# Second layer: the first 17 tiles listed from three sequences' counts, the last sequence routed within the stage; the prologue reordered; integers kept as integers in the rows

## The reference

```python
x = x + 0.5 * moe(layernorm(x))      # 8 experts, top 2 per token
x = x + lru(layernorm(x))            # complex diagonal recurrence over the sequence
x = x + 0.5 * moe(layernorm(x))

def moe(x):
    logits = x @ router_w.T + router_b
    topk_val, topk_idx = top_k(logits, 2)
    weights = softmax(topk_val)
    # expert e: h = x @ w1[e].T + b1[e]; h1, h2 = split(h); (silu(h1) * h2) @ w2[e].T + b2[e]
    return sum over the two chosen experts of weight * expert(x)
```

## Time and profile before

| | us |
|---|---|
| median of 3 runs | 672.25 (671.88 to 679.42) |
| the profiled run | 666.18, its span 664.4 |
| prologue, until the first expert matmul | 99.9 |
| first layer's tiles | 188.5 |
| recurrence and routing | 156.8 |
| second layer's tiles | 188.9 |
| outputs of the second layer | 30.3 |

### The profile page before, as it was taken

One profiled execution on the slowest core, in us unless ns is written; L12 is line 12 of the kernel. 1 busy time (PEld: TensorE's weight loads), 2 busy tenths in 40 slices (PEclk: granted clock), 3 DMA queues, 4 the chain that ended last, 5 costly groups with the idle time before them and its releaser, 6 DMA issues.

```text
span 664.4 us, 16357 instructions
## 1 busy us (share of the span) xinstructions
PE 462.8 (70%) x4580; PEld 408.6 (61%) x4580; DVE 423.0 (64%) x1336; ACT 350.9 (53%) x798; POOL 333.4 (50%) x463
## 2 busy tenths in 40 slices
PE   2433007888899999971988783327879799999910
PEld 2433005676699988860878673216769599989910
DVE  6563564656689996737799384145546477776715
ACT  4656233555577777752253431325457477877720
POOL 1277683545656655560002657604557556565640
PEclk9999999879899999985889786558889799999975
DMA  6142362333323222206000101102333223232228
GB/s 195 53 144 72 113 155 63 73 78 80 65 56 67 60 56 52 60 15 227 27 0 18 49 24 56 50 16 61 80 75 84 61 63 69 53 56 61 54 67 313
DMA packets 94552, 50.17 MB, mean 76 GB/s; under 512 B 81902, under 2 KB 84720, under 8 KB 94484
## 3 DMA queue, kind: packets, MB, share of 16 engines
q1 hardware_dynamic: 85396, 32.31, 20.3%
q0 software_dynamic: 9088, 16.94, 8.0%
HBM read 17.25 MB, written 23.24 MB: 61 GB/s over the span
## 4 chain that ended last, share of the span: by engine, by line
PE 55%; DVE 18%; issue 13%; DMA 5%; ACT 3%; another core or an unknown queue 3%; SPq 1%; POOL 1%; POOLq 0%; DVEq 0%; ACTq 0%
PE bank L1188 11%; PE bank L1189 11%; PE bank L1190 11%; PE bank L1210 5%; PE bank L1208 5%; PE bank L1209 5%; DMA yin<-y 3%; DVE bn L658 2%; DVE xres L909 2%; ACT xn L462 2%; PE bank L1070 1%; PE bank L1202 1%; PE bank L1168 1%; DVE w1l L786 1%
## 5 line engine op out<-in xcount | busy, mean ns | idle before, releaser
L424 POOL DMA_INDIRECT y<-yout,dest x156 | 155.3, 995 | 142.3 <-ACT yout L549 105.7
L993 DVE SCALAR_TENSOR_TENSOR act<-bank,bias,gate 128x256 f32<-128x256 f32 x312 | 146.3, 479 | 105.0 <-ACT gate L531 86.6
L403 POOL DMA_INDIRECT rows<-rows,slot_i x128 | 136.2, 1064 | 149.9 <-DVE slot_i L745 110.2
L1188 PE MATMUL bank<-xt_t,w1h 128*128 128x256 f16 x624 | 176.1, 282 | 26.9 <-DVE w2l L786 13.0
L531 ACT ACTIVATE gate<-bank,bias 128x256 f32<-128x256 f32 x312 | 142.3, 479 | 89.1 <-remote 56.0
L1190 PE MATMUL bank<-xt_t,w1l 128*128 128x256 f16 x624 | 175.7, 282 | 4.9 <-issue 4.9
L1189 PE MATMUL bank<-xt_t,w1h 128*128 128x256 f16 x624 | 175.8, 282 | 4.6 <-issue 4.3
L1210 PE MATMUL bank<-w2h,actl 128*128 x624 | 123.5, 223 | 5.8 <-issue 5.8
L1208 PE MATMUL bank<-w2h,wst 128*128 x624 | 124.9, 223 | 3.5 <-issue 3.0
L1209 PE MATMUL bank<-w2l,wst 128*128 x624 | 123.5, 223 | 2.7 <-issue 2.7
L999 DVE TENSOR_TENSOR actl<-act,wst 128x512 f16<-128x512 f32 x156 | 107.8, 691 | 15.2 <-ACT wst L539 10.3
(11 more groups left out here) (200 smaller groups left out, 552.9 us busy)
## 6 DMA issues: line engine op xcount, KB each, us to landing
yin<-y SPq DMA_DIRECT2D x16, 512.0 KB, 4.8
wst<-in_w_t SPq DMA_DIRECT2D x8, 512.0 KB
y<-yout,dest POOLq DMA_INDIRECT x156
rows<-padrow SPq DMA_DIRECT2D x18, 130.0 KB
xres<-in_x SPq DMA_DIRECT2D x8, 256.0 KB, 3.4
wst<-in_w_t SPq DMA_DIRECT2D x8, 256.0 KB
rows<-rows,slot_i POOLq DMA_INDIRECT x128
out<-xres SPq DMA_DIRECT2D x4, 512.0 KB, 6.8
```

What stands on the lines that cost most here:

```text
L403: pool.indirect_dma_start(out=rows_dram[f], out_offset=bass.IndirectOffsetOnAxis(ap=slot_i[:, k, f, g, t:t + 1], axis=0), in_=rows[:, k, g ...
L424: pool.indirect_dma_start(out=y_dram[f], out_offset=bass.IndirectOffsetOnAxis(ap=dest[:, t % STEP, r:r + 1], axis=0), in_=yout[:, t % STEP ...
L993: V.scalar_tensor_tensor(act[:, j, :], up_ps[j][:, SLOT:], bias[:, t % STEP, HB + j:HB + j + 1], gate[:, j, :], ALU.add, ALU.mult).then_in ...
L1188: T.matmul(o, w1h[:, bass.ds(at, P)], xt_t[:, t % STEP, 0, :], start=True, stop=False)
```

## The change

- **Routing of the second layer.** After the third sequence a first table is made from three sequences' counts; its first 17 tiles (`KNOWN`) are the list with which the stage begins. Of the last sequence VectorE's add, measure and scales and ScalarE's xn stay ahead of the stage. Its transposes (behind TensorE's tile 0), logits (2), rank (5) and list (10), ScalarE's copies (tiles 0, 1, 4) and VectorE's row parts, choose, weights, slots and table (eight linked steps in two places of each tile from tile 3 on) are in the stage. The exponential for its weights is made by VectorE in 17 steps. The nine pads of the second layer stand in SyncE's queue ahead of tile 17's load, behind the second list. The fourth sequence's `add_outputs` and `measure` are moved ahead of the loop over sequences.
- **GpSimd.** In both layers 42 rows are sent ahead of the tiles (48 + 6 before) and two with each of the tiles 0 to 10 (in the second layer 0 to 2 and 5 to 12).
- **Rows.** Destinations are stored as integer bits, so y's indirect DMA and ScalarE's weighting read meta directly, which has eight buffers; `take_meta` is gone.
- **Prologue.** Ten of the twelve small loads go behind the first four experts'; wst stages four experts; gate, act and the split activations share its memory. Statistics are made earlier, weight splits later.
- All engines' tiles are written out, without loops.

```diff
-PEEL = 6
-ROW_PEEL, LOAD_PEEL = 14, 18
-AHEAD = 6
+METAS = 8
+STAGED = 4
+AHEAD_2 = 10
+LATE = BATCH - 1
+RANKED, LISTED = 5, 10
 SEGS = BATCH * NE
 WHOLE = [(TOPK * SEQ * (g + 1) - NE * (SLOT - 1) + SLOT - 1) // SLOT for g in range(BATCH - 1)]
...
+KNOWN = WHOLE[LATE - 1]
...
-            return t_ps[0] if g == BATCH - 1 else rank_ps
+            return t_ps[0] if g == LATE else rank_ps
+        def logit_bank(f, g):
+            return t_ps[1] if (f, g) == (1, LATE) else logit_ps
...
+            return t_ps[1][0:1, SEGS:SEGS + NTILE] if n == 2 else list_ps[0:1, 0:NTILE]
...
+            for e in range(NE):
+                if e == STAGED:
                     for dst, src in small:
                         sp.dma_start(dst, src).then_inc(s_small, 16)
-            for e in range(NE):
-                if e >= 2:
-                    sp.wait_ge(s_wl, 2 * (e - 1))
-                sp.dma_start(wst[:, e % 2, 0:2 * HID], w1_t[:, e, :]).then_inc(s_w[e % 2], 16)
-                sp.dma_start(wst[:, e % 2, 2 * HID:], w2_t[:, e, :]).then_inc(s_w[e % 2], 16)
+                if e >= STAGED:
+                    sp.wait_ge(s_wl, 2 * (e - STAGED + 1))
+                sp.dma_start(wst[:, e % STAGED, 0:2 * HID], w1_t[:, e, :]).then_inc(s_w[e % STAGED], 16)
+                sp.dma_start(wst[:, e % STAGED, 2 * HID:], w2_t[:, e, :]).then_inc(s_w[e % STAGED], 16)
...
+                def load(t, n, dma):
+                    if f > 0 and t == KNOWN:
+                        sp.wait_ge(s_tab, 3)
+                        for e in range(NE):
+                            pad(e)
+                        pad_end()
+                    row0 = sp.value_load(toff_i[0:1, f, t:t + 1], min_val=0, max_val=NE * REG)
                     if t in FIRST_OF:
...
+                    wait(sp, s_ysent[t % STEP], dma(STEP - METAS, 32))
+                    sp.dma_start(meta[:, t % METAS, :, :],
                                  rows_dram[f][bass.ds(row0, SLOT), P:].rearrange("(r p) w -> p r w", p=P))\
...
+                    if f == 0 and STEP <= t < STEP + NE:
                         pad(t - STEP)
-                    if t == STEP + NE:
-                        sp.dma_start(rows_dram[f][NE * REG:NE * REG + SLOT, :].rearrange("(p r) w -> p r w", r=2),
-                                     padrow[:, :, :]).then_inc(s_pad, 16)
+                    if f == 0 and t == STEP + NE:
+                        pad_end()
...
-            def take_meta(t, n, dma):
-                pool.wait_ge(s_meta[t % STEP], dma(STEP, 16))
-                wait(pool, s_ysent[t % STEP], dma(0, 32))
...
-                pool.tensor_copy(dest[:, t % STEP, :], meta[:, t % STEP, :, 0])
-                pool.tensor_copy(weight[:, t % STEP, :], meta[:, t % STEP, :, 1]).then_inc(s_dest, 1)
...
-                        out_offset=bass.IndirectOffsetOnAxis(ap=dest[:, t % STEP, r:r + 1], axis=0),
+                        out_offset=bass.IndirectOffsetOnAxis(ap=meta_i[:, t % METAS, r, 0:1], axis=0),
...
+                each = [(g, i) for g in range(BATCH) for i in range(TOPK * GT)]
+                ahead = 2 * TOPK * GT + AHEAD_2
+                for g, i in each[:ahead]:
+                    send_row(f, g, i)
+                later = iter(each[ahead:])
...
+                def tile(t, n, dma):
+                    send_y(f, t, n)
+                    for g, i in islice(later, 0 if f > 0 and t in (3, 4) else 2):
                         send_row(f, g, i)
-                take_meta(0, lambda u: f * NTILE + u, lambda u, each: each * sent_before(f, u))
-                for i in range(AHEAD):
-                    send_row(f, BATCH - 1, i)
...
-                def tile(t, s, n, dma):
-                    if t + 1 < NTILE:
-                        take_meta(t + 1, lambda u: n(u + 1), lambda u, each: dma(u + 1, each))
-                    send_y(f, t, n)
-                    if t < TOPK * GT - AHEAD:
-                        send_row(f, BATCH - 1, AHEAD + t)
-                expert_tiles(pool, f, tile, ROW_PEEL)
...
+                act_e.wait_ge(s_b2, 2)
+                nc.scalar.mul(b2h[:, 1, 0:NE * P], b2h[:, 0, 0:NE * P], ident[0:2, 0:1]).then_inc(s_b2, 1)
             rows_of(0, 0)
             for g in range(BATCH):
                 if g + 1 < BATCH:
-                    rows_of(0, g + 1)
+                    normalise(number["ffn", 0, g + 1])
+                    high_part(0, g + 1)
+                    if g > 0:
+                        weight_high(g - 1)
+                    transposed(number["ffn", 0, g + 1])
+                else:
+                    second_bias()
+                    for e in range(BATCH - 2, NE - 3):
+                        weight_high(e)
                 exp_dif(0, g)
                 second_row(0, g)
...
-                act_e.wait_ge(s_dest, n(1))
+                act_e.wait_ge(s_meta[t % STEP], dma(STEP, 16))
...
+                if f > 0 and t == 0:
+                    high_part(1, LATE)
+                if f > 0 and t == 1:
+                    transposed(number["ffn", 1, LATE])
+                if f > 0 and t == 4:
+                    second_row(1, LATE)
...
-                    for g in range(BATCH):
+                    for g in range(LATE):
                         rows_of(1, g)
...
+                if f > 0:
+                    normalise(number["ffn", 1, LATE])
...
                 q = f * BATCH + g
-                dve.wait_ge(s_edif, q + 1)
+                if (f, g) == (1, LATE):
+                    yield from exponential(edif[:, q % 2, :], dif[:, q % 2, :], GT)
+                else:
...
+            together(measured(0))
+            together(scales(0, 1))
+            together(measured(1))
+            together(scales(1, 1), measured(2))
+            dve.wait_ge(s_route, 16 * 2)
+            row_parts(0, 0)
+            together(measured(3))
+            together(choose(0, 0), scales(2, 1))
+            weights_and_slots(0, 0)
+            row_parts(0, 1)
+            together(choose(0, 1), scales(3, 1))
+            weights_and_slots(0, 1)
+            weight_low(0)
+            row_parts(0, 2)
+            together(choose(0, 2))
+            weight_low(1)
+            weights_and_slots(0, 2)
+            row_parts(0, 3)
+            together(choose(0, 3))
+            together(tile_table(0, BATCH))
+            weight_low(2)
+            together(tile_list(0, 0, 0, NTILE))
+            dve.wait_ge(s_small, 16 * 10)
...
+            for e in range(3, NE):
+                weight_low(e)
+            tables, late = recurrence_tables(), None
...
+            def late_sequence():
+                row_parts(1, LATE)
+                yield 6
+                yield from choose(1, LATE)
+                yield
+                weights, places = row_weights(1, LATE), slots(1, LATE)
+                for chain in (weights, places):
+                    yield from chain
+                yield from tile_table(2, BATCH)
+                yield 99
+                yield from tile_list(2, 1, KNOWN, NTILE)
...
                 if f == 0 and t > 0:
-                    background(4)
+                    background(tables, 4)
+                if f > 0 and t > 2:
+                    background(late, 8)
...
                     recurrence(0)
+                    add_outputs(0, 3)
+                    measure(number["lru", 0, 3])
                     for g in range(BATCH):
...
                             recurrence(g + 1)
-                        if g == 0:
-                            add_outputs(0, 3)
-                            measure(number["lru", 0, 3])
-                        row_parts(1, g)
-                        together(choose(1, g))
-                        if g == BATCH - 1:
-                            tile_table(1)
-                            tile_list(1)
-                        if g == BATCH - 2:
-                            weights_and_slots(1, g)
-                expert_tiles(dve, f, lambda *tile_of: tile(f, *tile_of), NTILE if f == 0 else PEEL)
+                        if g < LATE:
+                            row_parts(1, g)
+                            together(choose(1, g))
+                        if g == LATE - 1:
+                            together(tile_table(1, LATE), row_weights(1, g), slots(1, g))
+                            together(tile_list(1, 1, 0, KNOWN))
...
-                    pe.wait_ge(s_entry, f + 1)
-                    T.matmul(list_ps[0:1, 0:NTILE], entry[:, :], ident[:, 0:NTILE],
-                             start=True, stop=True).then_inc(s_listed, 1)
+            def tile_row_of(n):
+                pe.wait_ge(s_entry, n + 1)
+                T.matmul(list_row(n), entry[:, :], ident[:, 0:NTILE], start=True, stop=True).then_inc(s_listed, 1)
...
-                        transpose_rows(number["ffn", 1, g])
-                        logits(1, g)
+                        if g < LATE:
+                            transpose_rows(number["ffn", 1, g])
+                            logits(1, g)
```

(8 more changed lines are left out.)

263 lines of the change are left out of this document (125 added, 138 removed).

## The result

The changed kernel takes 685.14 us (median of 20 runs, 674.78 to 693.16) against 674.56 (20 runs, 667.60 to 684.60): ratio 1.0136, interval 1.0099 to 1.0173. Some runs of every kernel are slower as a whole, and the ratios here leave out those over 1.5% above their kernel's fastest. It is slower, by less than the 2% inside which I had called it the same, and some 48 us above the 637 us forecast.

A forecast was written before the change was run, and what follows sets the result against it. The prediction saw order, buffers and late issues in the prologue and routing stretch as the bound, not work. Its terms, -19 + 3 - 3.5 - 22 + 5 + 3 + 5 - 3 - 1 = -32.5, led to 637 us, range 612 to 662.

The forecast's parts named there:

- the floor of 66: Prologue: earliest start of TensorE's expert matmuls, at 66 us without idle time, minus 34 against 99.86.
- I expect them again from 44 on [...]: 15 us: Prologue: late issues return over choose(0,3), the table and the splits, costing 15 us; tile 0 at about 81.
- the late issues: Engines starting late beside GpSimd's back-to-back indirect DMAs; in the old prologue they cost VectorE some 17 us.
- my upper bound of 91: Prologue: latest expected start of tile 0, at 91 us, minus 9, if the splits are drawn out as well.
- what it costs is that GpSimd pauses less: First stage: four indirect DMAs a tile, 5.1 us, stay below an early tile's 5.85; yout has four buffers; plus 3.
- My bound of plus 15: First stage: upper bound, plus 15 us if each of 11 tiles costs 1.4 us more.
- The routing stretch: Between the stages: minus 3.5 for add_outputs and measure moved, minus 22 for the list not awaiting the last sequence.
- The terms of the early list: Second stage: TensorE plus 5, VectorE plus 3, SyncE plus 5 and minus 3, unrolled loops minus 1.
- The pads' hole: Second stage: nine pads, 13 us, ahead of load 17 in SyncE's queue leave a hole at tile 17, plus 5.
- nothing, or a tile's delay: Second stage, GpSimd: send_row(1,3) waits at tile 5 for slots ready near tile 8; any delay is covered by yout.
- TensorE's term: Second stage: 8 transposes, 16 logit matmuls, count, rank and list in a full queue, plus 5 us.
- The one on the other side: Slower rival: GpSimd, never idle over 44 DMAs a stage, holds TensorE, 750 us; turning point 1.5 us a tile; chance 0.07.

The follow-up runs named there:

- a7: Changed kernel with its early list undone: the last sequence's routing stands ahead of the second stage again, pads with tiles 4 to 12; 695.24 us, 1.0341 to before.
- a3: Changed kernel with the first layer's rows as before, 54 ahead and one beside each of tiles 0 to 9; 651.66 us, 0.9794 to before.
- a0_after: The changed kernel itself, unaltered, run and profiled a second time; 683.91 us, 1.0145 to before.
- b1: The kernel before with a pause (memset and a wait for it) behind each row send only; 641.66 us, 0.9651 to before.
- a8: Changed kernel with its early list undone and a memset of 128 x 128 with a wait behind each row send; 662.25 us, 0.9858 to before.
- a4: Changed kernel with a memset of 128 x 128 and a wait behind each row send, none behind y sends; 649.62 us, 0.9648 to before.
- a9: Changed kernel with its early list undone and, in both layers, 54 rows ahead and one beside each of tiles 0 to 9; 681.82 us, 1.0146 to before.
- a2: Changed kernel with all 64 rows of the first layer sent ahead of its tiles, none beside them; 649.67 us, one run.
- c1: Changed kernel with 128 x 128 pauses behind all sends, eight yout and sixteen meta buffers, second-layer rows four a tile from tile 5; 642.71 us, 0.9546 to before.

## Why the prediction failed, point by point

- **The prologue** (-19 forecast, +6.8 measured) holds most of the error. The order did what it was to do: with the sends thinned out TensorE starts at 64.8 to 65.3, a microsecond from the floor of 66 that I had worked out, and 22 us ahead of the old order with its pause. The step that failed is "I expect them again from 44 on [...]: 15 us": against the paced kernels, which start at 65, the late issues cost 42 us here, 28.5 of them one wait for one semaphore. I had priced them by what they cost before (17 us). There VectorE went on at 72.83, while GpSimd paused by itself for 2.5 us, and I took the pause for what ends a hold. The 42 sends of the new order have no such pause, and here the hold outlasted them by 5 us. But a7's VectorE went on at 72.95 and a3's at 52.34 with the sends still under way, so what ends a hold is open. The six kernels of the new order without added pauses start their tiles at 83.1 to 113.1: 15 us is less than the least of them loses (18), and five pass my upper bound of 91.
- **The first stage** (+3, measured +16.6, in a0_after +13.7). The step "what it costs is that GpSimd pauses less" named the place and not the size. My bound of plus 15 was the right number; I took the lower value because 5.1 us of sends is less than the 5.85 of an early tile. What the traces show is that a delayed tile hands its y over together with the next, so that 4 DMAs in a row become 8, and tiles of 11 to 13 us stand beside these. That a send takes 1.44 us of the other engines, four of them 5.8 us of a tile of 4.07, was my reckoning from one hold, and the other prologues don't bear that figure out.
- **The routing stretch** (-25.5, measured -23.3 to its end, -18.8 to the first gated product, for which it was summed) holds, and a7 shows it by itself: -24.2. Inside it the details were off: the list came 11.7 us behind rank(1,2) (429.17 to 440.91), not 4, with VectorE waiting 10.45 us beside the 16 sends, and the first product 11 us behind the list, not 15 or more. And b1 shows what I hadn't seen: 22.7 us of the old stretch go with a pause alone. The two gains don't add up: with pauses the early list gives 19.8 us of stretch (a8 against a4), but a4's stretch is only 7.4 below b1's.
- **The second stage** (+9, measured +24.5). The terms of the early list sum to +9, and a7 measures 9.7. The pads' hole is there: they take 10.7 us of SyncE's queue, the next load goes 9.8 us later, and the tile lasts 8.9 us, close to the 5 us on top of 4.07. What I left out is the second row beside a tile, for which I had put "nothing, or a tile's delay": a7 and a9 put 16.9 us on it. One reading in TensorE's term was wrong: I gave the 16 logit matmuls 3.6 us at the lower clock and 2.3 at the higher, but in the trace of before they take 3.58 us at a granted 0.50 and 3.55 to 3.58 at 1.00 (all four in the prologue).
- **The rivals.** The one on the other side named the culprit, GpSimd's 44 DMAs a stage, with 1.5 us a tile as its turning point; over the first 15 tiles it was 1.1 us (6.83 us each in the first stage against 5.75), and my ground against it, that GpSimd pauses once TensorE slows, was half true: it pauses for 3 to 5 us and then has a double load. It missed the prologue, where the sign was decided.

Sum with the sizes measured: +6.8 + 16.6 - 23.3 + 24.5 - 0.7 = 24 between the two traces, 18 with a0_after, 11 between the medians.

Not settled: by which path GpSimd's DMAs hold a semaphore of TensorE's, what ends a hold, and why the same prologue came out at 106.7, 106.2, 99.9, 93.9 and 83.1 us in kernels that differ only behind its 42nd send, and at 83.1 and 113.1 in two that don't differ before the 48th (a3, a9). Within a kernel it repeats (106.7 and 106.2; the four runs of a3 and of a9 lie within 5 us each), so it goes with the program and not with chance. A hold by rate alone doesn't give these numbers. Taking a row's bytes or its number of descriptors down, which would tell what the rate is a rate of, wasn't tried.

## What to carry over

A wait that no record ends, beside an engine that issues DMAs without a pause, is a cost that belongs to the issuing engine's rhythm: before moving such work earlier or closer together, ask how long its longest run becomes, not how much of it there is. Here a memset of 0.2 to 0.3 us behind each send, on an engine that was thought too busy, was worth 3.5% on the kernel before and 5% on the changed one (649.62 us against 683.91). And don't price such a stall by its length in one trace: in six kernels with the same sends it was 6 to 36 us. Look first whether it can be had away altogether.

## What the chip showed that I had not expected

- A semaphore that TensorE's matmul raises was acted on 34.5 us late (50.63 to 85.15, 28.5 of them waiting) while GpSimd issued 42 indirect DMAs of 128 rows 1.27 us apart. In six kernels with sends 1.27 us apart this wait was 6.1 to 36.1 us; in seven with a mean distance of 1.46 us or more there was none.
- Sends beside the tiles hold ScalarE too: 16 in a row had it start 10.2 us after TensorE's products were done (a2). How dense they may be there isn't known: in c1, with about 1.5 us a send, GpSimd's own 6.5 us a tile stand in the way of telling.
- VectorE kept one of GpSimd's sends out for 7.8 us with operations that overlapped without a gap; gaps of 0.04 us ended that.
